# Two layers with causal attention on one core: row sums and values in one product, and the maxima on ScalarE's queue

## The chip, the core and the metric

The kernel runs on 1 core of one Trainium2 chip. The metric is device time in microseconds (us), the median over runs of the whole program.

## What is computed

Two layers, each an attention-like part and a feed-forward part. The change touches only the first of these parts, causal attention over 8 sequences of 512 tokens with 16 heads (32 of each head's query elements, 16 of them rotated):

```
q = concat(q_sem, rope(q_geo));  k likewise;  v = x @ Wv.T
scores = einsum('bhqd,bhkd->bhqk', q, k) * scale
scores = where(causal, scores, finfo.min)
attn   = softmax(scores, axis=-1)
out    = einsum('bhqk,bhkd->bhqd', attn, v)  ->  reshape(B, S, 256) @ Wo.T
```

## The kernel before

The program is a row of phases (layer norm, attention, layer norm, feed-forward, gates, state space and so on), each with a block per engine and a barrier at its end. The phase of the change is `causal_attention`. Its work is cut into 16 **halves** (batch b, f = 0 or 1: 8 heads each), and a half into 4 steps t, one **pair** of heads per step. All engines run the same `step(b, f, t, n)` in the same order. The order is written by hand: the calls inside `step` are each engine's queue, and each engine works through it in order.

For one pair, the work runs as follows.

- **Scores and maxima**, two steps ahead. PE's `scores` (L374, L377) makes scores with the query on the partitions, in three fills j = 0, 1, 2 of `p_s`. DVE's `maximum` (L573) takes the negated row maxima. POOL splits them in two (L347, L349). One step ahead, DVE's `turn_maxima` (L587) transposes them, and SP's `maxima_out` (L267) writes them to DRAM; `maxima_in` (L277, four transfers) reads them back as extra rows of the query tile `qs`.
- **Scores again, turned**, in the pair's own step. PE's `turned_scores` (L384) has the key on the partitions, and the extra rows subtract the maximum. It also comes in three fills of one buffer `p_st`: turned fill j, then DVE's `keep_past` (L580, the causal edge), then ACT's `exponential` (L522) into `pt_a`, `pt_b` or `pt_c`, and only then turned fill j + 1. Fill 0 of the next pair waits for the third exponential and for the maxima.
- **Values**. For a quad (4 heads, two pairs) PE's `weigh` (L414) multiplies the exponentials by `v_pad` into `p_o`, and by `ones` into `p_sum`: 16 products each per quad, each into 32 of the 128 partitions. `v_pad` has a head's 16 values in 16 columns and zeros in the other 16; both quads of a half add into the same `p_o` and `p_sum`. Fill 0 comes at t = 1 (quad 0) and t = 3 (quad 1), fills 1 and 2 at t = 2 and at t = 0 of the next half.
- **Normalisation**. At t = 0 of the next half DVE takes two reciprocals of `p_sum` (L625, L633) and multiplies into `ot` (L636).
- **Output**. For a finished batch PE's `project_out` (L422) runs at t = 3 and t = 2 of the next batch's first half, and DVE adds the residual (L600).

Beside this PE projects q, k and v of later halves (L48 to L50), DVE and POOL rotate them (L594, L325, L329), ACT copies them (L527, L552, L543), and SP writes them to DRAM (`spread_rows`, L255) and reads them back stacked by head (`stack`, L262: two transfers of 384 KB for q at t = 0, two for k at t = 1).

## Time and profile before

| | us |
|---|---|
| median of 3 runs (6273.44 to 6284.51) | 6275.0 |
| the profiled execution, its own time | 6271.5 |
| its span in the trace | 6269.7 |
| attention: first to last product with `ot` | 162.1 to 795.5 |
| PE busy, whole span | 5619.0 (90%) |
| DVE busy | 4504.9 (72%) |
| ACT busy | 3469.1 (55%) |
| POOL busy | 3610.0 (58%) |

The shares are means over phases with different limits. The phase of the change is a tenth of the span, so it is read by its own stretch, from about 62 us to 804 us. In the trace a matmul of fp32 counts as two records, so 4 products stand as "x8".

### The profile page before, as it was taken

Reading aid. Unit: us, or ns where it says so; the run is one execution under the profiler, and the core shown is the slowest. Engines: PE = TensorE matmul, PEld = TensorE weight load, DVE = VectorE, ACT = ScalarE, POOL = GpSimd, SP = SyncE. Lnnn points to the kernel's source line nnn. Section 1 sums busy time; section 2 is a strip of 40 time slices with the busy share of each in tenths; the row PEclk is TensorE's granted clock in tenths of the full one; section 3 lists DMA queues with packets and bytes.
Section 4 is the critical chain, followed back from the end, with each engine's and each line's share of the span. In section 5 each row is a group of like instructions: output and inputs, shape, how many; then the busy total and the mean of one; then the engine's idle time right before and its main releaser. Section 6 shows DMA issues by size and latency. Waiting matters only on the chain. (4 is left out here: it accounts for less than half of the span.)

```text
span 6269.7 us, 129594 instructions
## 1 busy us (share of the span) xinstructions
PE 5619.0 (90%) x41820; PEld 4006.3 (64%) x41820; DVE 4504.9 (72%) x6855; ACT 3469.1 (55%) x4692; POOL 3610.0 (58%) x4085
## 2 busy tenths in 40 slices
PE   5888858747999999999999999999999999985599
PEld 3444447535777777777777777777777777763487
DVE  4666555545888888888888888888888888844444
ACT  2233222134777777777777777777777777731122
POOL 2111100005888888888888888888888888830000
PEclk8899779868999999999999999999999999987799
DMA  3333210122111111111111111111111111122100
GB/s 91 91 93 84 68 61 24 47 71 66 31 28 33 29 30 28 32 29 30 29 30 32 28 31 28 32 29 30 28 33 29 30 28 31 29 77 74 42 24 20
DMA packets 428605, 263.10 MB, mean 42 GB/s; under 512 B 264740, under 2 KB 359524, under 8 KB 427652
## 3 DMA queue, kind: packets, MB, share of 16 engines
q1 hardware_dynamic: 420100, 253.98, 15.7%
q10 hardware_dynamic: 8448, 8.39, 0.4%
...
## 5 line engine op out<-in xcount | busy, mean ns | idle before, releaser
L1537 ACT ACTIVATE ss_r<-ss_pssum,ss_eps 128x512 f32<-128x512 f32 x512 | 352.8, 689 | 900.5 <-PE ss_pssum L1468 900.5
L1597 DVE SCALAR_TENSOR_TENSOR ss_psb<-ss_psb,ss_norm,ss_r 128x512 f32<-128x512 f32 x512 | 362.8, 754 | 446.2 <-ACT ss_r L1539 446.2
L1468 PE MATMUL ss_pssum<-ss_sq,ss_pairssum 128*128 128x512 f32 x1024 | 570.9, 639 | 57.1 <-DVE ss_fr L1585 57.0
L1349 POOL TENSOR_TENSOR ss_sq<-ss_sq 128x512 f32<-128x512 f32 x256 | 329.7, 1288 | 452.5 <-ACT ss_sq L1546 452.5
L48 PE MATMUL ss_psb<-x_hi,ss_whi 128*128 x1024 | 529.5, 517 | 4.4 <-DVE ss_fr L1585 4.4
L1449 PE MATMUL ss_psse<-ss_rot 64*128 64x128 f32 x8224 | 529.4, 279 | 1.2 <-POOL ss_rot L1331 1.2
L1379 POOL TENSOR_TENSOR ss_own<-ident,ss_tk 128x512 f32<-128x512 f32 x512 | 524.8, 1047 | 0.0
L1449 PEld LDWEIGHTS ss_psse<-ss_rot 64*128 64x128 f32 x8224 | 480.1, 188 | 44.4 <-issue 42.9
L48 PE MATMUL ss_psc<-x_hi,ss_whi 128*128 x1024 | 504.9, 493 | 0.0
L50 PE MATMUL ss_psb<-x_hi,ss_wlo 128*128 x1024 | 404.1, 395 | 0.0
L49 PE MATMUL ss_psc<-x_lo,ss_whi 128*128 x1024 | 403.6, 394 | 0.0
L1339 POOL TENSOR_TENSOR ss_sq<-ss_sq 128x512 f32<-128x512 f32 x256 | 325.1, 1270 | 135.0 <-ACT ss_sq L1553 135.0
L50 PE MATMUL ss_psc<-x_hi,ss_wlo 128*128 x1024 | 402.2, 393 | 0.0
L49 PE MATMUL ss_psb<-x_lo,ss_whi 128*128 x1024 | 402.0, 393 | 0.0
L1304 POOL MEMSET ss_rot<- 128x4096 f32 x1 | 3.5, 3512 | 669.5 <-POOLq L2018 669.5
L1458 PE MATMUL ss_psm<-ss_xe,ss_bt 128*128 128x16 f32 x3084 | 388.9, 264 | 0.0
L1458 PEld LDWEIGHTS ss_psm<-ss_xe,ss_bt 128*128 128x128 f32 x3084 | 363.9, 191 | 31.2 <-issue 0.2
L1597 DVE SCALAR_TENSOR_TENSOR ss_psc<-ss_psc,ss_norm,ss_r 128x512 f32<-128x512 f32 x512 | 361.5, 752 | 0.0
L1619 DVE TENSOR_TENSOR ss_gm<-ss_psse,ss_dec 128x1024 f32<-128x1024 f32 x257 | 314.7, 1224 | 41.7 <-POOL ss_dec L1340 41.7
L1539 ACT ACTIVATE ss_r<-ss_r 128x512 f32<-128x512 f32 x512 | 324.1, 633 | 16.3
L1373 POOL TENSOR_TENSOR ss_rot<-ss_rot,ss_tmp 128x512 f32<-128x512 f32 x256 | 333.0, 1301 | 0.0
L1519 ACT ACT_TABLE_LOAD x257 | 329.7, 1283 | 4.5
...
## 6 DMA issues: line engine op xcount, KB each, us to landing
...
a_qs<-head_rows SPq DMA_DIRECT2D x32, 384.0 KB, 5.7
a_ks<-head_rows SPq DMA_DIRECT2D x32, 384.0 KB, 5.6
...
```

The costliest lines, as they stand in the source:

```text
L48: nc.tensor.matmul(out, w_hi, x_hi, start=first, stop=False)
L49: nc.tensor.matmul(out, w_hi, x_lo, start=False, stop=False)
L50: return nc.tensor.matmul(out, w_lo, x_hi, start=False, stop=last)
L1349: G.tensor_tensor(sq[:, 0, 0], sq[:, 0, 0], sq[:, 0, 1], ALU.add).then_inc(ss_b, 1)
L1373: G.tensor_tensor(rot[:, j, 0], rot[:, j, 0], tmp[:, 0, 0], ALU.add)
L1379: last = G.tensor_tensor(own[:, h * TPB:(h + 1) * TPB], g.ident[:].rearrange("p (o t) -> p o t", o=1).broadcast_to([P, TPB, P]), at_diagon ...
L1449: last = M(p_se[:, h * TPB + c, :], rot[at, 1 - j, e, cols], rot[at, 1 - j, 2 + e, cols], start=e == 0, stop=e == 1)
L1458: last = M(p_m[:, (c * 2 + e) * PW:(c * 2 + e + 1) * PW], bt[:, 2 if e else j, c, :], xe[:, 1 - j, c, :], start=True, stop=True)
L1468: M(p_sum[:], pairs_sum[:], sq[:, q, 0], start=True, stop=True).then_inc((sum_b, sum_c)[q], 1)
L1519: A(trig[:, j, 0], fr[:], ACT.Sin, scale=UNDER_TURN)
L1537: A(r[:, q], p_sum[:], ACT.Ln, scale=1.0 / N1, bias=eps[:, 0:1]).then_inc(ln, 1)
L1597: link.mark(S(bank[:, e, :], bank[:, e, :], norm[:, 2 * q + e:2 * q + e + 1], r[:, q], ALU.mult, ALU.mult))
```

## The change

- `v_pad` is filled with ones where it was filled with zeros. One product then gives a head's values in 16 of its 32 partitions and its row sums in the other 16. The `ones` products and `p_sum` are gone, and each quad has its own `p_o` buffer.
- ACT's new `take` copies a quad's `p_o` twice to SBUF: plain (`o_sb`), and scaled by a column `own` of ones and zeros that keeps only the value rows (`o_own`). It comes at t = 3 for quad 0 and at t = 0 of the next half for quad 1.
- SP's new `gather_sums` moves the sum rows of `o_sb` by four transfers of 32 KB to the partitions that hold the values (`sums`).
- POOL adds the two `o_own` at t = 1 into `o_all`. DVE takes the first reciprocal at the end of t = 1, the second in t = 2 ahead of `keep_past` 2, and multiplies into `ot` at the end of t = 2.
- `maxima_out` and `maxima_in` move from SP's queue to ACT's, between exponentials 0 and 1. The four transfers in become two, of two rows each. DVE turns the maxima before `maximum` 0 and not after it.
- `stack` and `spread_rows` no longer stand behind the maxima on SP's queue.
- `project_out` moves from t = 3 and t = 2 of half f = 0 to t = 3 of f = 0 and t = 0 of f = 1. ACT's two copies into `v_pad` come before exponential 0.

```diff
         vt, v_pad = sb("vt", [P, SEQ]), sb("vpad", [P, TPB, 2, 2, 4, 2 * DH])
-        ones, nil = sb("ones", [P, 2, 2 * DH]), sb("nil", [P, 2, TPB])
+        nil = sb("nil", [P, 2, TPB])
+        o_sb, sums = sb("osb", [P, 2, SEQ]), sb("sums", [P, SEQ])
+        o_own, o_all = sb("oown", [P, 2, SEQ]), sb("oall", [P, SEQ])
+        strips, own = sb("strips", [P, 2, 4]), sb("own", [P, 2])
...
-        p_o, p_sum = ps("o", [P, SEQ]), ps("sum", [P, SEQ])
+        p_o = [ps(f"o{q}", [P, SEQ]) for q in range(2)]
...
             for t in range(4):
                 step(BATCH, 0, t, BATCH)
+            step(BATCH, 1, 0, BATCH)
...
-            def maxima_out(b, g_next):
-                p = g_next % 2
-                sp.wait_ge(turned_done, b * 8 + g_next + 1)
-                sp.dma_start(max_dram[p], trn[:, p, :]).then_inc(max_out[p], 16)
-
-            def maxima_in(b, g_next):
-                p = g_next % 2
-                f, u = g_next // 4 % 2, g_next % 4
-                sp.wait_ge(max_out[p], (b * 4 + g_next // 2 + 1) * 16)
-                columns = max_dram[p].rearrange("(a c) r -> c a r", a=TPB)
-                for e in range(2):
-                    for s in range(2):
-                        at = 64 * e + KS + s
-                        sp.dma_start(qs[at:at + 1, f, u, :].bitcast(FP32).rearrange("o (i a r) -> o i a r", i=TPB, a=TPB),
-                                     columns[8 * e + 4 * s:8 * e + 4 * s + 4].unsqueeze(0)).then_inc(max_in[p], 16)
+            def gather_sums(half, quad):
+                sp.wait_ge(o_copied, half * 2 + quad + 1)
+                for c in range(4):
+                    to, at = 32 * c + DH * quad, 32 * c + DH * (1 - quad)
+                    sp.dma_start(sums[to:to + DH, :], o_sb[at:at + DH, quad, :]).then_inc(sums_in, 16)
 
             def step(b, f, t, n):
...
                 half = 2 * n + f
                 after = (b, 1) if f == 0 else (b + 1, 0)
-                if is_pair(4 * half + t + 1):
-                    maxima_out(b, 4 * f + t + 1)
-                if t < 2 and is_half(half + 1):
-                    stack(*after, t)
-                if is_pair(4 * half + t + 1):
-                    maxima_in(b, 4 * f + t + 1)
                 if t == 0 and is_half(half + 1):
+                    stack(*after, 0)
                     spread_rows(*after, 1)
+                if t == 1 and is_half(half + 1):
+                    stack(*after, 1)
                 if t == 2 and is_half(half + 2):
                     spread_rows(b + 1, f, 0)
-                if f == 1 and t == 0 and 1 <= n < BATCH:
+                if t == 3 and is_half(half):
+                    gather_sums(b * 2 + f, 0)
+                if t == 0 and is_half(half - 1):
+                    gather_sums(b * 2 + f - 1, 1)
+                if f == 1 and t == 1 and 1 <= n < BATCH:
                     before = b - 1
...
-            G.memset(v_pad[:], 0.0).then_inc(cleared, 1)
+            G.memset(v_pad[:], 1.0).then_inc(cleared, 1)
...
+                if t == 1 and is_half(half - 1):
+                    pool.wait_ge(o_masked, (b * 2 + f) * 2)
+                    at_least(pool, ot_done, b * 2 + f - 1)
+                    G.tensor_tensor(o_all[:], o_own[:, 0], o_own[:, 1], ALU.add).then_inc(merged, 1)
...
-                    for psum, left in ((p_o, lambda c: v_pad[:, kt, f, quad, c, :]), (p_sum, lambda c: ones[:, quad, :])):
-                        for c in range(4):
-                            last = M(psum[32 * c:32 * c + 32, kt * P:SEQ], left(c), pt[:, c // 2, c % 2, at:at + width],
-                                     start=quad == 0 and j == 0, stop=quad == 1 and j == 2, skip_group_check=True)
+                    for c in range(4):
+                        last = M(p_o[quad][32 * c:32 * c + 32, kt * P:SEQ], v_pad[:, kt, f, quad, c, :], pt[:, c // 2, c % 2, at:at + width],
+                                 start=j == 0, stop=j == 2, skip_group_check=True)
...
-                outs = f == 0 and 1 <= n <= BATCH
+                outs = 1 <= n <= BATCH
...
-                if t == 3 and outs:
+                if f == 0 and t == 3 and outs:
                     if is_half(half + 1):
                         pe.wait_ge(vpad_done, b * 2 + f + 2)
                     pe.wait_ge(ot_done, b * 2)
-                    project_out(b, 1, c)
+                    project_out(b, 0, c)
                 if t == 3 and is_half(half + 2):
-                    if outs:
-                        pe.wait_ge(res_done, b * 2 - 1)
...
                 if earlier:
                     pe.wait_ge(exp_done, pairs_done * FILLS)
                     weigh(ef, eq, 2)
+                if f == 1 and t == 0 and outs:
+                    if is_half(half + 1):
+                        pe.wait_ge(rope_read, counts(1) + 4)
+                    pe.wait_ge(res_done, b * 2 - 1)
+                    project_out(b, 1, c)
                 if t == 1 and is_half(half + 2):
                     at_least(pe, rope_read, counts(1) + 4)
+                    if f == 1 and outs:
+                        pe.wait_ge(res_done, b * 2)
                     project(b + 1, f * HALF + P, c).then_inc(proj_done, 1)
-                if t == 2 and outs:
-                    if is_half(half + 2):
-                        pe.wait_ge(rope_read, counts(2) + 1)
-                    if is_half(half + 1):
-                        pe.wait_ge(vt_ready, b * 2 + f + 2)
-                    at_least(pe, res_done, b * 2 - 2)
-                    pe.wait_ge(ot_done, b * 2)
-                    project_out(b, 0, a)
                 if t == 3 and is_half(half + 2):
-                    if outs:
-                        pe.wait_ge(res_done, b * 2)
+                    if f == 0 and outs:
+                        pe.wait_ge(res_done, b * 2 - 1)
...
                     pe.wait_ge(exp_done, pairs_done * FILLS + 1)
                     if t == 1:
                         pe.wait_ge(vpad_done, b * 2 + f + 1)
-                        at_least(pe, ot_done, b * 2 + f)
+                    at_least(pe, o_masked, b * 4 + f * 2 - 1 + t // 2)
                     weigh(f, t // 2, 0)
...
+            def take(half, quad):
+                act.wait_ge(pv_done, (half * 2 + quad + 1) * FILLS)
+                at_least(act, rec_done, half)
+                at_least(act, merged, half)
+                A(o_sb[:, quad], p_o[quad][:], ACT.Copy).then_inc(o_copied, 1)
+                A(o_own[:, quad], p_o[quad][:], ACT.Copy, scale=own[:, quad:quad + 1]).then_inc(o_masked, 1)
+
+            def maxima_out(b, g_next):
+                p = g_next % 2
+                act.wait_ge(turned_done, b * 8 + g_next + 1)
+                act.dma_start(max_dram[p], trn[:, p, :]).then_inc(max_out[p], 16)
+
+            def maxima_in(b, g_next):
+                p = g_next % 2
+                f, u = g_next // 4 % 2, g_next % 4
+                act.wait_ge(max_out[p], (b * 4 + g_next // 2 + 1) * 16)
+                columns = max_dram[p].rearrange("(a c) r -> c a r", a=TPB)
+                for e in range(2):
+                    at = 64 * e + KS
+                    act.dma_start(qs[at:at + 2, f, u, :].bitcast(FP32).rearrange("s (i a r) -> s i a r", i=TPB, a=TPB),
+                                 columns[8 * e:8 * e + 8].rearrange("(s i) a r -> s i a r", s=2)).then_inc(max_in[p], 16)
...
-                if here:
-                    exponential(b, f, t, 0)
-                if t == 0 and is_half(half + 1):
-                    high(*after, 1)
-                if t == 2 and is_half(half + 2):
-                    high(b + 1, f, 0)
...
                 if t == 3 and is_half(half + 1):
                     act.wait_ge(vt_done, b * 2 + f + 2)
...
                 if here:
+                    exponential(b, f, t, 0)
+                if is_pair(4 * half + t + 1):
+                    maxima_out(b, 4 * f + t + 1)
+                if t == 0 and is_half(half + 1):
+                    high(*after, 1)
+                if t == 2 and is_half(half + 2):
+                    high(b + 1, f, 0)
+                if is_pair(4 * half + t + 1):
+                    maxima_in(b, 4 * f + t + 1)
+                if here:
                     exponential(b, f, t, 1)
                     exponential(b, f, t, 2)
+                if t == 3 and here:
+                    take(b * 2 + f, 0)
+                if t == 0 and is_half(half - 1):
+                    take(b * 2 + f - 1, 1)
...
-                V.tensor_tensor(rows, p_ab[part][:].rearrange("p (n d) -> p n d", n=2), rows, ALU.add).then_inc(res_done, 1)
+                V.tensor_tensor(rows, p_ab[1][:].rearrange("p (n d) -> p n d", n=2), rows, ALU.add).then_inc(res_done, 1)
...
-                outs = f == 0 and 1 <= n <= BATCH
+                outs = 1 <= n <= BATCH
                 here = is_half(half)
                 if here:
                     keep_past(b, f, t, 0)
+                if is_pair(4 * half + t + 1):
+                    turn_maxima(b, 4 * f + t + 1)
                 if ahead:
                     maximum(b, f, t, 0)
-                if is_pair(4 * half + t + 1):
-                    turn_maxima(b, 4 * f + t + 1)
-                if t == 3 and outs:
-                    add_residual(b, 1)
+                if f == 0 and t == 3 and outs:
+                    add_residual(b, 0)
                 if here:
                     keep_past(b, f, t, 1)
                 if t % 2 and is_half(half + 2):
...
                     maximum(b, f, t, 1)
                 if t % 2 and is_half(half + 2):
                     turn(b + 1, f, t // 2, 1)
-                if t == 0 and is_half(half - 1):
-                    dve.wait_ge(pv_done, (b * 2 + f) * 2 * FILLS)
-                    V.reciprocal(rec[:, 0:SEQ // 2], p_sum[:, 0:SEQ // 2])
+                if f == 1 and t == 0 and outs:
+                    add_residual(b, 1)
+                if t == 2 and is_half(half - 1):
+                    V.reciprocal(rec[:, SEQ // 2:SEQ], sums[:, SEQ // 2:SEQ]).then_inc(rec_done, 1)
                 if here:
                     keep_past(b, f, t, 2)
-                if t == 2 and outs:
-                    add_residual(b, 0)
                 if ahead:
                     maximum(b, f, t, 2)
-                if t == 0 and is_half(half - 1):
-                    V.reciprocal(rec[:, SEQ // 2:SEQ], p_sum[:, SEQ // 2:SEQ]).then_inc(rec_done, 1)
+                if t == 1 and is_half(half - 1):
+                    dve.wait_ge(sums_in, (b * 2 + f) * 128)
+                    at_least(dve, ot_done, b * 2 + f - 1)
+                    V.reciprocal(rec[:, 0:SEQ // 2], sums[:, 0:SEQ // 2])
+                if t == 2 and is_half(half - 1):
                     at_least(dve, wo_done, b * 2 if f else b * 2 - 2)
+                    dve.wait_ge(merged, b * 2 + f)
                     dve.wait_ge(rec_done, b * 2 + f)
-                    V.tensor_tensor(ot[:, 1 - f, :], p_o[:], rec[:], ALU.mult).then_inc(ot_done, 1)
+                    V.tensor_tensor(ot[:, 1 - f, :], o_all[:], rec[:], ALU.mult).then_inc(ot_done, 1)
 
             batches(dve, step)
```

Two places show how the queues move. First ACT, in the loop's second half (f = 1) at t = 0, from exponential 0 on (after, as far as the copies of `p_o`); `a_pta`, `a_ptb` and `a_ptc` are the outputs of exponentials 0, 1 and 2. Before:

```order
L522 ACTIVATE a_pta<-a_psst 128x1024 [waits a0_pv]
L525 REGISTER_ALU
L527 ACTIVATE a_yhi<-a_y 128x512 [waits a0_kspread,ln0_loaded6]
L518 REGISTER_ALU
L218 REGISTER_ALU [waits a0_keep]
L522 ACTIVATE a_ptb<-a_psst 128x1024 [waits a0_pv]
...
L522 ACTIVATE a_ptc<-a_psst 128x512 [waits a0_pv]
L550 REGISTER_ALU
L552 ACTIVATE a_vt<-a_psa 128x512 [waits ln0_normed,ln0_var]
```

After:

```order
L518 ACTIVATE a_pta<-a_psst 128x1024 [waits a0_pv]
L529 REGISTER_ALU
L530 DMA maxima<-a_trn 128x32 [waits a0_turned]
L543 REGISTER_ALU
L545 ACTIVATE a_yhi<-a_y 128x512 [waits a0_kspread,ln0_loaded6]
L539 DMA a_qs<-maxima 2x16x32 [waits a0_maxout1]
L539 DMA a_qs<-maxima 2x16x32
...
L518 ACTIVATE a_ptb<-a_psst 128x1024 [waits a0_pv]
...
L518 ACTIVATE a_ptc<-a_psst 128x512 [waits a0_pv]
L521 ISA
L524 ACTIVATE a_osb<-a_pso 128x512 [waits a0_merged,a0_rec,a0_pv]
L525 ACTIVATE a_oown<-a_pso,a_own 128x512
```

Exponential 1 now stands behind three DMA issues and a wait for the first of them to land, and two copies of `p_o` stand behind exponential 2.

Second SP, in the same half at t = 0. Before:

```order
L267 DMA maxima<-a_trn 128x32 [waits a0_turned]
L259 ISA
L262 DMA a_qs<-head_rows 48x4x512 [waits a0_qspread]
L262 DMA a_qs<-head_rows 48x4x512
L277 DMA a_qs<-maxima 1x16x32 [waits a0_maxout1]
L277 DMA a_qs<-maxima 1x16x32 x3
```

After, from `gather_sums` of the step before:

```order
L272 DMA a_sums<-a_osb 16x512 [waits a0_ocopied]
L272 DMA a_sums<-a_osb 16x512 x3
L263 ISA
L266 DMA a_qs<-head_rows 48x4x512 [waits a0_qspread]
L266 DMA a_qs<-head_rows 48x4x512
```

The maxima no longer follow the two stacked transfers on one queue.

## Rows read from the trace of the kernel before

**Rows 1.** The tile `a_ot`: the multiplication that ends each of the 16 halves

```profile
L636 DVE TENSOR_TENSOR a_ot<-a_pso,a_rec x16: 691/692/693, 162.1 to 795.5; 128x512 f32<-128x512 f32 x16
```

**Rows 2.** Stages: length, busy time (instructions) of PE, PEld, DVE, ACT, POOL; clock, DMA

```profile
162.00:795.50 633.50, 547.79 (x3862) 284.43 (x3862) 373.19 (x635) 184.42 (x244) 88.61 (x166) 0.87 0.34 81
```

**Rows 3.** Waits from 157 to 700 us: total, times, longest

```profile
PE a_psst L384 <- DMA a_qs<-maxima: 50.8, 26, 3.4
```

**Rows 4.** Timeline of PE, a step t = 0: start, length, instruction, idle before it

```profile
363.19 1.04 PE L414 MATMUL a_pssum<-a_pta,a_ones 128*32 128x512 f32 x8
...
364.17 0.50 PE L384 MATMUL a_psst<-a_qs,a_ks 50*128 50x512 f32 x2
...
366.34 0.83 PE L414 MATMUL a_pssum<-a_ptb,a_ones 128*32 128x384 f32 x8
366.98 0.40 PE L414 MATMUL a_pso<-a_ptb,a_vpad 128*32 128x128 f32 x8
367.20 0.40 PE L414 MATMUL a_pssum<-a_ptb,a_ones 128*32 128x128 f32 x8
367.53 0.50 PE L384 MATMUL a_psst<-a_qs,a_ks 50*128 50x384 f32 x4
...
369.06 0.61 PE L414 MATMUL a_pssum<-a_ptc,a_ones 128*32 128x256 f32 x8
370.03 0.39 PE L384 MATMUL a_psst<-a_qs,a_ks 50*128 50x256 f32 x2 [0.35 <-ACT a_ptb L522]
...
375.74 0.72 PE L384 MATMUL a_psst<-a_qs,a_ks 50*128 50x512 f32 x2 [3.20 <-DMA a_qs<-maxima]
```

**Rows 5.** Timeline of ACT, the same step

```profile
365.28 1.03 ACT L522 ACTIVATE a_pta<-a_psst 128x1024 f32<-128x1024 f32 x1 [1.98 <-DVE a_psst L580]
368.95 1.02 ACT L522 ACTIVATE a_ptb<-a_psst 128x1024 f32<-128x1024 f32 x1 [2.13 <-DVE a_psst L580]
372.07 0.60 ACT L522 ACTIVATE a_ptc<-a_psst 128x512 f32<-128x512 f32 x1 [2.09 <-DVE a_psst L580]
372.65 0.60 ACT L552 ACTIVATE a_vt<-a_psa 128x512 f32<-128x512 f32 x1
```

**Rows 6.** Timeline of DVE, the same step, and POOL's operation of the added one's size

```profile
366.90 1.28 POOL L329 TENSOR_TENSOR a_ylo<-a_y,a_yhi 128x512 fp32r<-128x512 f32 x1 [2.78 <-ACT a_yhi L527]
...
369.88 1.75 DVE L625 RECIPROCAL a_rec<-a_pssum 128x256 f32<-128x256 f32 x1
...
371.55 0.41 DVE L580 TENSOR_TENSOR a_psst<-a_psst,a_limit 128x256 f32<-128x256 f32 x1
```

**Rows 7.** Timeline of SP's queue, the same step (DMA issues)

```profile
367.30 0.32 SPq L267 DMA_DIRECT2D maxima<-a_trn  x1
367.75 0.83 SPq L262 DMA_DIRECT2D a_qs<-head_rows  x2
368.72 2.58 SPq L277 DMA_DIRECT2D a_qs<-maxima  x4
```

**Rows 8.** Timeline near the phase's end, with no stacked transfer in flight

```profile
775.19 0.32 SPq L267 DMA_DIRECT2D maxima<-a_trn  x1
776.62 2.55 SPq L277 DMA_DIRECT2D a_qs<-maxima  x4
...
780.71 0.21 PEld L384 LDWEIGHTS a_psst<-a_qs,a_ks 50*128 50x128 f32 x2 [1.42 <-DMA a_qs<-maxima]
```

**Rows 9.** Stages of 3 us around that step, columns as in rows 2

```profile
374.00:377.00 3.00, 1.26 (x6) 0.64 (x6) 1.33 (x3) 0.04 (x1) 0.00 (x0) 0.81 0.66 236
377.00:380.00 3.00, 3.00 (x11) 1.97 (x11) 1.41 (x3) 0.99 (x1) 0.00 (x0) 0.50 0.00 0
398.00:401.00 3.00, 1.93 (x11) 1.30 (x11) 1.84 (x4) 1.58 (x3) 0.35 (x2) 0.79 0.19 71
```

**Rows 10.** DMA issues: size and time from issue to landing

```profile
a_qs<-head_rows SPq DMA_DIRECT2D x32, 384.0 KB, 5.7
```

**Rows 11.** Timeline of PE, an output projection at full clock

```profile
393.89 1.99 PE L422 MATMUL a_psa<-a_wo,a_ot 128*128 128x256 f32 x8
```

19 lines of the change are left out of this document (11 added, 8 removed).

## The prediction

> **What bounds the kernel now.** I read the tile `a_ot` first, for the period. Its multiplication ends a half, and 16 of them lie between 162.1 and 795.5 us [rows 1]: 633.4 us for 15 periods, 42.2 us for a half of four steps. The stage's busy times come next [rows 2]: PE 547.8 of 633.5 us, DVE 373, ACT 184, POOL 89. Per half PE is busy for 547.8/15 = 36.5 us and idle for 5.7, at a mean granted clock of 0.87, between its levels 1.2 and 2.4 GHz. PE is the engine that the others wait for, and its idle time says what it waits for itself. The longest of it ends with a maxima transfer: 50.8 us in 26 waits from 157 to 700 us [rows 3], which is 26 waits in some 13 halves, two per half and 3.9 us.
>
> The timelines of one step t = 0 show why. I count from its start T = 364.17 [rows 4]. Turned fill 0 runs at T, exponential 0 ends at T + 2.14 [rows 5], turned fill 1 starts at T + 3.36, exponential 1 ends at T + 5.80, turned fill 2 starts at T + 5.86. The next step starts at T + 11.57, after 3.20 us of waiting for the maxima [rows 4]. On SP's queue [rows 7] the write of the maxima is issued at 367.30, two stacked transfers at 367.75, and the four transfers in from 368.72 to 371.30. They reach PE 4.44 us later (375.74). Near the phase's end nothing stacked is in flight, and the same transfers, issued until 779.17, release PE at 780.71 [rows 8]: 1.54 us. So the stacked transfers, 5.7 us to land [rows 10], hold up the small ones behind them by 2.9 us. After such a wait the clock falls: 0.81, then 0.50 in the next stretches [rows 9]. A busy share of only 1.93 in 3 us already goes with 0.79 [rows 9].
>
> **The sums leave PE.** Per quad they are four groups of products. By start to next start they take 0.98 (363.19 to 364.17), 0.64 (366.34 to 366.98) and 0.33 us (367.20 to 367.53), and the last at most 0.61 [rows 4]: 2.56 in all. A tenth or so of each group is its drain, which the values' products then show instead, so I take 2.3 per quad, 4.6 per half at full clock. Divided by the clock of 0.87 it would be 5.3. I take 4.8. PE busy per half: 36.5 − 4.8 = 31.7 us.
>
> **The maxima on ACT's queue.** ACT now stands still from exponential 0 to exponential 1. From the write's issue to the first issue in it was 1.42 us (367.30 to 368.72) and 1.43 [rows 7, 8]. An issue in takes 2.58/4 = 0.64 [rows 7], so two take 1.29. The block is B = 2.71 us. The trace shows no two-row issue; a stacked one takes 0.42 [rows 7], so the pair lies between 0.83 and, if the price goes by rows, 2.58: B between 2.25 and 4.0. I take 2.71, since the form is nearest to the old one. The turning comes before `maximum` 0 now, so the write needn't wait for it. ACT's copy `y_hi` lies inside the wait.
>
> In the step above exponential 1 can start at T + 2.14 + 2.71 = T + 4.85, against T + 4.78 before, and turned fill 2 at T + 5.93. PE reaches that point at 5.51 without its wait of 0.35, less the sums of 0.97 and 0.5: T + 4.04. So **1.9 us of the freed PE time turns into a wait for ACT**. What follows: keep 0.41 and exponential 0.60 end by T + 7.5, where they ended at 8.50 behind the reciprocal of 1.75 [rows 5, 6]. PE's rest of the step is 2.5 us, so it ends at T + 8.45. The maxima are issued by T + 4.85 and land 1.54 later if nothing holds them up: the wait of 3.2 is gone.
>
> Step t = 2 has the same chain and the same idle of 1.9. The first reciprocal, at the end of t = 1, delays its `keep_past` 0 by about 1.1 (1.75 against a gap of some 0.65); the second fits into DVE's slack. At t = 1 and t = 3 projections keep PE busy until turned fill 2, and the later exponential costs some 0.15 each. One of two output projections, 1.93 us [rows 11], moves into the idle time of t = 0 in every second half: −0.95 per half. PE idle per half: 1.9 + 1.9 + 1.1 + 0.3 − 0.95 = 4.25.
>
> **What else is added.** Four copies of `p_o` per half, 0.60 each [rows 5], stand behind exponential 2 at t = 0 and t = 3 (1.2 us, at t = 0 with `a_vt` 1.8). The next exponential 0 is needed 1.1 us after the next T, which lies about 1 us after exponential 2: it is hidden, and costs up to 0.8 per step if steps get as short as 7.5. POOL's addition, 1.28 us [rows 6] on an engine that is busy for 89 us of 633, is hidden before `total`. If it weren't, the rotation of q would be late, not the chain. The gathers are 4 issues (1.7 us) and a landing on SP, and are waited for at the end of t = 1, some 4 us later; if late, all of DVE stands behind that wait. The moved stacked transfer of k waits for the gather at the end of t = 0 and is issued at about 1.4 us into t = 1, where it was 3.4 before, and needed only at t = 2.
>
> **The sum.** Period: 31.7 + 4.25 = 35.95 us, 6.25 less. Over 15 periods that is −94. Half 0 ahead of them gives −6. The tail gets longer: copy 0.6, issues 1.7, landing 1.5, less the last sums: +3. In all −97, from 6271.5 (the profiled execution) to 6174.5. The median of the runs is 3.5 above that execution, so **6178 us**. Changes within 0.2% (12.5 us) can't be told from none.
>
> **Rivals.**
>
> *The clock comes back too.* At full clock in all of the stage, 36.5 us of busy time is about 0.87 × 36.5 = 31.8, less 4.6 = 27.2, plus 4.25 = 31.4: −160. Halfway there is 6145. For: the waits of 3.2 go. Against: idle shares of 4.25 in 36 are hardly below 5.7 in 42, and rows 9 show a fall after less. Chance 0.14.
>
> *The maxima stay late on their new queue.* If the landing of 4.44 us stays wherever a stacked transfer is in flight (t = 0 and t = 1), the maxima are there at T + 9.3, 0.8 after the end of t = 0 and 1.5 after that of t = 1 (about 7.75 long). That is 2.3 per half, +35: 6213. For: ACT's queue has no engines of its own in any row, and stacks go out before the maxima now. Against: the landing of 1.54 is that of transfers with an empty queue before them. The Trainium skill (DMA: Bandwidth & Descriptors, Issuing engines are not separate DMA queues) says that DMAs of all queues run on the same 16 engines and interleave, and that another queue only saves issue time. By that rule the time would be this rival's; the trace of before has these transfers on one queue only and can't tell. The same page (Why a DMA increments its semaphore by 16 and not by 1) says that a transfer spreads over as many engines as divide its slowest dimension. That would be 2 for the two-row form, and points the same way; no run here shows it yet. Chance 0.12.
>
> *ACT is blocked for longer.* A step of the bare chain takes 2.14 + B + 1.08 + 1.6 = 4.84 + B. With B = 4.3 the steps are 10.0 (with the projection of v), 9.15, 10.25 and 9.15, with 0.3 for the outputs: 38.9 per half, −50, so 6222. Chance 0.09.
>
> *The change is slower, by the same place.* The chain rules all steps then: a half is 21.7 + 4B us, which is 42.2 from B = 5.1 on. With B = 6, when the write of the maxima lands behind the stacked transfers as these land themselves (5.7 us less what has passed), 45.7 per half give +54: 6330. For: the stacked transfers are now issued just ahead of that write. Against: at 2 of 4 steps nothing is in flight, and B of 1.42 + issues was the same in both places of [rows 7, 8]. Chance 0.07.
>
> *The removed products buy nothing* (PE only waits longer) and the gain is the maxima's 3.9 us alone: 6275 − 58 = 6217. Against: PE has no wait at t = 1 and t = 3 before turned fill 2. Chance 0.04.
>
> **How the numbers follow.** The forecast, 6150 to 6205, has 0.54. The range of 6120 to 6232 takes in most of the faster clock and the three weaker gains. Faster by over 0.2%: 0.54 + 0.14 + 0.12 + 0.09 + 0.04 = 0.93, less 0.01 for a weak case that ends near no change. Slower has 0.06 of the 0.07, same 0.02.
>
> **What would show it.** Right: no `a_pssum` rows; 36 us between `a_ot` rows; maxima waits on PE far below 50.8 us; PE waiting for `a_ptb` at t = 0 and t = 2 for about 1.9 us each; exponential 1 about 2.7 us after the end of exponential 0. Wrong: an issue of the two-row transfer above 1 us, 1.42 grown to over 2, maxima waits at t = 0 and t = 1, or DVE waiting for `a_sums`. The forecast falls if B is over 3.5 us or the granted clock leaves 0.87 by more than 0.05.

## The result, and the profile after

| | median us | lowest to highest | runs |
|---|---|---|---|
| before | 6276.06 | 6273.44 to 6284.51 | 4 |
| after | 6235.38 | 6233.29 to 6247.79 | 4 |

The ratio is 0.9936, 95% interval 0.9924 to 0.9949: 40.7 us faster, where 97 were forecast. The time lies above the range of 6120 to 6232. The profiled execution of after is the slowest of its four runs: its own time is 6247.8 us, its span 6245.8. Against the profiled execution of before (6271.5) that is only 23.7 us less, so the readings below explain 23.7 us and not 40.7.

The tile `a_ot` of after and the stage between its first and last multiplication (length, then busy time and instructions of PE, PEld, DVE, ACT, POOL; clock, DMA share, GB/s):

```profile
L667 DVE TENSOR_TENSOR a_ot<-a_oall,a_rec x16: 679/681/693, 175.2 to 768.0; 128x512 f32<-128x512 f32 x16
```

```profile
175.20:768.00 592.80, 515.00 (x2806) 270.62 (x2806) 362.73 (x614) 211.12 (x298) 109.84 (x177) 0.76 0.38 89
```

That is 592.8/15 = 39.5 us, against 42.2 [rows 1], at a clock of 0.76 in place of 0.87. But the two stages don't hold the same work. `a_ot` is now made two steps later in the half: its first multiplication comes 13.1 us later and its last 27.5 us earlier, so the stage of after leaves out two full steps at its start and takes in two nearly empty ones at its end. The stage from the first exponential 0 to the last, 63 steps or 15.75 halves, is the same stretch of the work in both, but for the products taken out. Before, then after:

```profile
112.48:781.75 669.27, 581.43 (x4074) 303.14 (x4074) 397.51 (x678) 198.22 (x264) 97.46 (x184) 0.88 0.35 84
112.94:752.07 639.13, 563.77 (x3084) 296.48 (x3084) 398.00 (x678) 230.80 (x324) 121.83 (x199) 0.77 0.39 93
```

| per half, us | before | after |
|---|---|---|
| length | 42.5 | 40.6 |
| PE busy | 36.9 | 35.8 |
| PE idle | 5.6 | 4.8 |
| clock of the stage | 0.88 | 0.77 |
| busy time times clock | 32.5 | 27.6 |

So a thousand TensorE instructions fewer are only 1.1 us per half less busy time. Busy time times clock fell by 4.9: the work did leave, and most of what it freed came back as slower products.

What PE waited for in after, 157 to 700 us (total, times, longest), the row of [rows 3] and its neighbours:

```profile
PE a_psst L383 <- DMA a_qs<-maxima: 26.2, 17, 2.8
PE a_psst L383 <- ACT a_ptb L518: 24.3, 21, 3.7
PE a_psst L383 <- ACT a_ptc L518: 7.1, 10, 0.8
```

The waits for maxima halved (50.8 in 26 before). In their place stand waits for exponential 1. A step t = 0 of after on PE, where [rows 4] were read before (start, length, instruction, idle before it):

```profile
357.38 0.50 PE L383 MATMUL a_psst<-a_qs,a_ks 50*128 50x512 f32 x2
...
359.88 0.50 PE L383 MATMUL a_psst<-a_qs,a_ks 50*128 50x384 f32 x4
...
361.07 0.64 PE L412 MATMUL a_pso<-a_ptc,a_vpad 128*32 128x256 f32 x8
362.68 0.39 PE L383 MATMUL a_psst<-a_qs,a_ks 50*128 50x256 f32 x2 [0.97 <-ACT a_ptb L518]
...
364.81 0.63 PE L50 MATMUL a_psa<-x_hi,a_wlo 128*128 x1
...
367.57 0.50 PE L383 MATMUL a_psst<-a_qs,a_ks 50*128 50x512 f32 x2 [0.90 <-DMA a_qs<-maxima]
```

The same step on ACT and, below, on SP's queue (issues have a q):

```profile
358.51 1.02 ACT L518 ACTIVATE a_pta<-a_psst 128x1024 f32<-128x1024 f32 x1 [0.58 <-DVE a_psst L608]
358.59 0.36 ACTq L530 DMA_DIRECT2D maxima<-a_trn  x1
...
360.13 1.28 ACTq L539 DMA_DIRECT2D a_qs<-maxima  x2
361.60 1.02 ACT L518 ACTIVATE a_ptb<-a_psst 128x1024 f32<-128x1024 f32 x1 [1.55 <-DVE a_psst L608]
```

```profile
357.37 2.43 SPq L272 DMA_DIRECT2D a_sums<-a_osb  x4
360.28 0.82 SPq L266 DMA_DIRECT2D a_qs<-head_rows  x2
```

The step is 367.57 − 357.38 = 10.2 us long, 11.57 before. Turned fill 2 waits 0.97 us for exponential 1. The write of the maxima is issued 0.08 us after exponential 0 starts, not at its end, so exponential 1 starts 2.07 us after that end (359.53). The two reads of the maxima are issued in 1.28 us, until 361.41, and reach PE at 367.57, which is 6.16 us later. SP was held by the gathers, so the stacked q goes out at 360.28, into the same time.

The clock after such short waits is the main reading. The stretches around one step, columns as in rows 2, and the waits there:

```profile
336.00:339.00 3.00, 3.00 (x26) 1.08 (x23) 3.00 (x6) 0.53 (x2) 1.07 (x3) 1.00 0.00 0
340.00:342.80 2.80, 1.55 (x16) 0.58 (x17) 2.42 (x4) 1.32 (x2) 1.28 (x1) 0.96 0.12 41
342.80:346.00 3.20, 3.20 (x13) 1.79 (x14) 2.74 (x4) 1.21 (x3) 0.78 (x2) 0.50 1.00 324
346.00:350.00 4.00, 4.00 (x14) 2.58 (x14) 1.83 (x4) 1.07 (x2) 0.00 (x0) 0.50 0.15 47
350.00:354.00 4.00, 4.00 (x14) 2.40 (x13) 2.49 (x4) 1.02 (x1) 0.00 (x0) 0.50 0.01 1
```

```profile
339.83 0.51 PE L383 MATMUL a_psst<-a_qs,a_ks 50*128 50x384 f32 x4 [0.41 <-ACT a_pta L518]
...
342.80 0.58 PE L383 MATMUL a_psst<-a_qs,a_ks 50*128 50x256 f32 x2 [1.25 <-ACT a_ptb L518]
...
348.19 0.63 PE L49 MATMUL a_psa<-x_lo,a_whi 128*128 x1
348.62 0.63 PE L50 MATMUL a_psa<-x_hi,a_wlo 128*128 x1
...
369.40 0.40 PE L49 MATMUL a_psa<-x_lo,a_whi 128*128 x1
369.64 0.39 PE L50 MATMUL a_psa<-x_hi,a_wlo 128*128 x1
```

The clock is full from 336 us on. Two waits of 0.41 and 1.25 us come, with work between them, and then at least 11 us at 0.50 in which PE never stops. The projections of the step run in them: a projection product takes 0.63 us and the next starts after 0.43, where it is 0.40 and 0.24 at full clock (369.40). By that ratio the 11.2 us (342.80 to 354.00) would be 6.3 at full clock, so I estimate that some 5 us go for 1.7 us of waiting, if nothing else would have held the step up. Not each wait does this: after the one of 0.41 the clock stayed at 0.96 up to the next wait. The Trainium skill (TensorE: Matmul & The Clock Gate, A second HAM failure mode: psum-queue depth-cycling) tells of a kernel whose clock oscillates since PE is idle for short times between its groups of matmuls, often enough. This trace agrees, with 1.00, 0.96 and 0.50 in the stretches above.

### The profile page after: what moved, and what is told of

Same layout as the page of the kernel before. It is cut to its first block and busy times, and to the rows that moved or that the text cites. A ratio compares the mean times of both kernels' runs of the same rounds, so it can differ in the third digit from the quotient of the medians.

```text
span 6245.8 us, 127791 instructions
## 1 busy us (share of the span) xinstructions
PE 5602.4 (90%) x40796; PEld 4001.3 (64%) x40796; DVE 4506.1 (72%) x6856; ACT 3504.9 (56%) x4756; POOL 3632.0 (58%) x4101
## 5 line engine op out<-in xcount | busy, mean ns | idle before, releaser
L1404 POOL TENSOR_TENSOR ss_rot<-ss_rot,ss_tmp 128x512 f32<-128x512 f32 x256 | 332.7, 1300 | 0.0
L1405 POOL TENSOR_TENSOR ss_rot<-ss_rot,ss_tmp 128x512 f32<-128x512 f32 x256 | 332.5, 1299 | 0.0
```

Source lines behind the costliest of these rows:

```text
L1404: G.tensor_tensor(rot[:, j, 0], rot[:, j, 0], tmp[:, 0, 0], ALU.add)
L1405: G.tensor_tensor(rot[:, j, 1], rot[:, j, 1], tmp[:, 0, 1], ALU.add).then_inc(rot_b, 1)
```

## The experiments

Eighteen kernels ran, 0.2% (12.5 us) again being what can be told. "before" was run beside each (its medians lie between 6274.9 and 6277.8). PE's waits, busy times and clocks below are of the stretch from 162 to 700 us where nothing else is said; for after that is 478.16 us busy at 0.78, for before 474.05 at 0.89.

One correction holds for several expectations. The phase has 16 halves (the 16 multiplications of `a_ot`), and the expectations of e9 and e12 count 28 to 32. The sums' products are 4.6 x 16 = 74 us of PE work, e12 and e13 leave out 60% of that, 44 us, and the time at which "work off is time off" would put e12 is 6230. The sixteen zero-weight products per place are 1.93 us long there at full clock, 62 us in all over 32 places (e16's row below), and not 1.03 each time as e16's expectation says.

**e1_zeros_back.** PE's work as before, in the new order.

```diff
-                    for c in range(4):
-                        last = M(p_o[quad][32 * c:32 * c + 32, kt * P:SEQ], v_pad[:, kt, f, quad, c, :], pt[:, c // 2, c % 2, at:at + width],
-                                 start=j == 0, stop=j == 2, skip_group_check=True)
+                    for left in (lambda c: v_pad[:, kt, f, quad, c, :], lambda c: zero[:]):
+                        for c in range(4):
+                            last = M(p_o[quad][32 * c:32 * c + 32, kt * P:SEQ], left(c), pt[:, c // 2, c % 2, at:at + width],
+                                     start=j == 0 and first, stop=j == 2, skip_group_check=True)
+                        first = False
```

> The changed kernel, and behind each group of value products the same number of products with weights of zero into the same place: PE does as much work as before the change, the result stays. Theory (the clock): removing the sums' products left PE too idle in places and the clock fell from 0.87 to 0.78 in this phase, which ate the saving. Then the granted clock of the phase returns to 0.85 or more and the time stays within 15 us of the changed kernel's 6235, or falls. Rival (PE's work counts and the clock falls for another reason, such as ACT's block): the clock stays near 0.78 and the time rises by the products' 4.6 us per half or more, 75 us, to 6310.

Measured: 6247.3 us (6242.9 to 6251.5), ratio 0.9952, interval 0.9939 to 0.9966. The clock is 0.91, PE's busy time 479.4 us. Putting back 74 us of PE work costs 12 us against after, which is within what can't be told from nothing, and brings the clock back from 0.78. This is the pair that puts back exactly what the change took.

**e2_fill_wait.** 16 zero-weight products of 256 columns ahead of fill 2 of the values, at t = 0 and t = 2, where PE waits next for exponential 1.

```diff
+            def fill_wait(quad):
+                for _ in range(4):
+                    for c in range(4):
+                        M(p_o[quad][32 * c:32 * c + 32, 2 * P:SEQ], zero[:], pt_c[:, c // 2, c % 2, :],
+                          start=False, stop=False, skip_group_check=True)
...
                     pe.wait_ge(exp_done, pairs_done * FILLS)
+                    fill_wait(eq)
                     weigh(ef, eq, 2)
```

> The changed kernel, and 16 products of 256 columns with weights of zero only at t = 0 and t = 2, before fill 2 of the values, where PE waits 1.25 us for exponential 1; some 1.8 us of PE at full clock. Theory (the clock falls in the stretches after that wait): the clock of the phase rises to 0.9, the slow stretches after t = 0 and t = 2 shrink, and the period goes from 39.5 to about 37 us: some 40 us less, 6195. Rival (ACT's block sets the period): the filler costs nothing and brings nothing, or costs up to 0.6 us twice per half: 6235 to 6255.

Measured: 6220.8 us (6218.6 to 6222.1), ratio 0.9909, interval 0.9894 to 0.9925. The clock is 0.88. More work on the busiest engine, and 14.6 us less than after; it lies between the two times that I had given.

**e3_max_sp.** The maxima back on SP, the write ahead of the stacked transfers and the read behind them as before, the rest as after.

```diff
-                act.dma_start(max_dram[p], trn[:, p, :]).then_inc(max_out[p], 16)
+                sp.dma_start(max_dram[p], trn[:, p, :]).then_inc(max_out[p], 16)
...
+                if is_pair(4 * half + t + 1):
+                    maxima_out(b, 4 * f + t + 1)
+                if t < 2 and is_half(half + 1):
+                    stack(*after, t)
+                if is_pair(4 * half + t + 1):
+                    maxima_in(b, 4 * f + t + 1)
```

> The changed kernel with the maxima back on SP's queue (write, stacked transfers, two two-row transfers in, as before); values and sums in one product and the spread normalisation stay. Theory of the maxima's queue: the waits for the maxima return to 3 to 4 us per half, ACT's block goes, PE idles more and the clock falls to 0.75 or less: 6255 to 6280, no better than before the change. Rival (the maxima on ACT cost more by the block than they gain): faster than 6235.

Measured: 6236.3 us (6226.9 to 6243.1), ratio 0.9932, interval 0.9919 to 0.9946: as after. My expectation missed. With the sums gone, taking the maxima back to SP, in the old order with the stacked transfers, makes no difference in sum. PE waits more for them (35.0 us from 162 to 740, after 26.2) and less for exponential 1 (17.7 against 25.6): what ACT's block costs is what SP's queue costs.

**e4_sibling.** Before, with the other half of the change: maxima on ACT and read by two transfers of two rows, turned ahead of `maximum` 0, stacks no longer behind them on SP, ACT's copies into `v_pad` ahead of exponential 0. Products with ones, the normalisation and the place of the output projections stay old. The main lines of the edit:

```diff
-                sp.dma_start(max_dram[p], trn[:, p, :]).then_inc(max_out[p], 16)
+                act.dma_start(max_dram[p], trn[:, p, :]).then_inc(max_out[p], 16)
...
-                    maximum(b, f, t, 0)
                     turn_maxima(b, 4 * f + t + 1)
+                    maximum(b, f, t, 0)
```

> The kernel before with the maxima on ACT's queue, the turning first and the stacked transfers free of them, but with the products by ones and the old normalisation. Theory (the clock): PE has its 4.6 us more per half, so its waits are short, the clock is above 0.87, and the time is 6230 to 6245, close to the changed kernel: the removed products gave next to nothing. Rival (the sums' removal is what gives the 41 us): 6265 or more.

Measured: 6218.6 us (6217.0 to 6231.1), ratio 0.9912, interval 0.9899 to 0.9926: 59 us off before (6277.8 in that comparison), and 17 us faster than the whole change. It is faster than I expected under either theory. So these edits alone bring more than the whole change, and the rest of it (the sums' part and the moved projections) costs time on top of them. In 162 to 740 us PE waits 0.3 us for maxima (before 55.4), 45.4 for exponential 1.

**e12_drop_sums.** Before, without the products with ones for key tiles 1 to 3. It is the forecast's first term by itself.

```diff
                     for psum, left in ((p_o, lambda c: v_pad[:, kt, f, quad, c, :]), (p_sum, lambda c: ones[:, quad, :])):
+                        if psum is p_sum and kt > 0:
+                            continue
```

> The kernel before with nothing changed but this: the products with ones are left out for key tiles 1 to 3 (768 of 1280 columns, so 60 percent of what the change takes off TensorE, 2.9 us of 4.8 per half); the sums then hold key tile 0 only. Order, waits, queues and normalisation stay. If work off TensorE comes off the period at an unchanged clock: 32 halves x 2.9, some 80 to 90 us less over 28 to 32 halves, 6190 to 6200. If the clock gives it back, as e1 and e2 suggest: 6255 to 6285, with a clock in 162 to 740 of 0.82 or less in place of 0.89.

Measured: 6295.1 us (6287.4 to 6295.9), ratio 1.0033, interval 1.0020 to 1.0046. 44 us of work are left out and the kernel is 20 us **slower**, more than even the clock theory gave it; its clock, 0.85, is above the 0.82 that I had named. PE waits and a stretch of e12 (waits of 157 to 700 us; PE's timeline; stages):

```profile
PE a_psst L384 <- DMA a_qs<-maxima: 68.6, 33, 4.6
PE a_psst L384 <- ACT a_ptb L524: 13.7, 19, 0.8
```

```profile
381.55 0.49 PE L384 MATMUL a_psst<-a_qs,a_ks 50*128 50x512 f32 x2 [3.90 <-DMA a_qs<-maxima]
...
384.67 0.63 PE L50 MATMUL a_psa<-x_hi,a_wlo 128*128 x1
```

```profile
377.00:381.50 4.50, 0.65 (x3) 0.19 (x1) 3.12 (x4) 1.09 (x2) 0.40 (x2) 1.00 1.01 251
381.50:385.00 3.50, 3.45 (x13) 2.19 (x14) 1.66 (x4) 1.02 (x1) 0.00 (x0) 0.56 0.02 9
385.00:389.00 4.00, 4.00 (x14) 2.20 (x14) 1.83 (x6) 0.85 (x1) 0.00 (x0) 0.50 0.59 105
389.00:392.00 3.00, 3.00 (x12) 1.64 (x10) 1.58 (x3) 0.17 (x1) 0.00 (x0) 0.50 0.86 130
```

The waits for maxima grew from 50.8 to 68.6 us, those for exponential 1 from 6.6 to 13.7: 25 us more of waiting in 13 of the 16 halves. The wait of 3.90 is followed by 10 us at half clock, and the clock of the stage fell from 0.89 to 0.85. The products with ones stood in the time in which the maxima are on their way.

**e5_stack_first and e6_stack_fill.** After, with the stacked transfers ahead of the gathers on SP (gathers at t = 0 and t = 1, and a wait for the last turned scores in place of the order that the gathers gave); e6 adds the products of e2.

```diff
                 if t == 0 and is_half(half + 1):
+                    at_least(sp, st_done, (b * 8 + 4 * f) * FILLS)
                     stack(*after, 0)
+                if t == 0 and is_half(half - 1):
+                    gather_sums(b * 2 + f - 1, 0)
...
+                if t == 1 and is_half(half - 1):
+                    gather_sums(b * 2 + f - 1, 1)
```

> The changed kernel with SP's issues of t=0 and t=1 in another order: the stacked transfers of q (384 KB) ahead of the gathers of sums, which move from t=3 and t=0 to t=0 and t=1. Theory A (part of what is missing is the collision of the late-issued stacked transfer with the maxima, because four gather issues of 0.61 us hold SP ahead of it): write to read-issue gaps on ScalarE's queue fall from up to 5.0 to about 1.5 us, TensorE's waits for maxima in 162 to 740 from 26 us to under 12 us, time 6215 to 6230. Theory B (only TensorE's clock decides; the waits for exponentials leave it at 0.76 to 0.78 whatever SP does): 6232 to 6240 and clock of 162 to 740 unchanged.

> The order of e5 together with the sixteen zero-weight products ahead of fill 2 of the values at t=0 and t=2 (e2, 6220.8 by itself). If transfers and clock are two separate losses, the gains add: about 15 us of the clock and what e5 brings, 6195 to 6215, with a clock of 0.88 or above in 162 to 740. If the two are the same loss (a wait that was filled cannot be shortened again): 6216 to 6224.

Measured: e5 6278.0 us (6269.3 to 6282.6), ratio 1.0002, interval 0.9993 to 1.0011; e6 6204.4 us (6200.6 to 6205.6), ratio 0.9886, interval 0.9871 to 0.9901. e5 is 43 us above after and neither theory had it; e6 lies in the 6195 to 6215 that I gave it, but not for the reason given, since e5 brings nothing that could be added. PE no longer waits for maxima at all from 162 to 740 us, and waits 63.6 us for exponential 1 (after 25.6). The same place of e5 on ACT, and on SP:

```profile
359.61 1.02 ACT L520 ACTIVATE a_pta<-a_psst 128x1024 f32<-128x1024 f32 x1
359.69 0.35 ACTq L532 DMA_DIRECT2D maxima<-a_trn  x1
...
364.73 1.28 ACTq L541 DMA_DIRECT2D a_qs<-maxima  x2
```

```profile
357.00 0.81 SPq L266 DMA_DIRECT2D a_qs<-head_rows  x2
```

From the write's end of issue to the read's issue pass 4.69 us, where it was 1.1: the write of 16 KB lands while the stacked 384 KB, issued 2.7 us ahead, are in flight, and ACT stands still until it has. In 13 of e5's 14 or so halves from 162 to 740 us there is one such gap of 4.3 to 4.95 us. In after there are three over 4 us in 57 steps (4.17 to 4.68), and each has a stacked k issued 0.01 to 0.16 us before the write; two more, of 3.36 and 3.48, have the four gathers just issued. Before the change no gap of 56 is over 1.23. One of after's three:

```profile
410.59 1.02 ACT L518 ACTIVATE a_pta<-a_psst 128x1024 f32<-128x1024 f32 x1 [1.84 <-DVE a_psst L608]
410.70 0.36 ACTq L530 DMA_DIRECT2D maxima<-a_trn  x1
415.23 1.26 ACTq L539 DMA_DIRECT2D a_qs<-maxima  x2
416.66 1.02 ACT L518 ACTIVATE a_ptb<-a_psst 128x1024 f32<-128x1024 f32 x1 [5.05 <-issue]
```

```profile
410.69 0.81 SPq L266 DMA_DIRECT2D a_ks<-head_rows  x2
```

The Trainium skill (DMA: Bandwidth & Descriptors, Issuing engines are not separate DMA queues) says that transfers of all issuing engines run on the same 16 engines and interleave. These rows agree: another engine's queue did not take the small transfer past the large one.

e6 shows the other half: the same order with 62 us of filler is 73.6 us faster than e5, at a clock of 0.93 against 0.76. It has as many gaps over 4 us as e5 (13), and e4 has twelve over 3 us, with a stacked transfer issued 3.5 to 5 us before, and both are faster than after. So a gap isn't dear by itself; it is dear where PE has little else to do.

**e7_zeros_stack.** e1 in the order of e5 (the edits of both, shown above).

> e1 (zero-weight products behind each group of values, TensorE's work as before, 6247.3) with the stacked transfers ahead of the gathers. e1 and the sibling form e4 (6218.6) have the same work on TensorE and differ by 29 us in how the normalisation is done and when. If the place of the gathers on SP explains that difference: 6215 to 6228. If it is the rest of the normalisation (ScalarE's copies of rows, the reciprocals and the earlier end of it): 6240 to 6250.

Measured: 6266.0 us (6254.7 to 6273.5), ratio 0.9983, interval 0.9973 to 0.9992: neither. Moving the gathers behind the stacks costs here too, 19 us over e1. So they are not cured by a new place. Set beside e6, it also shows that the place of PE work counts for more than its amount: both have the same order, e7 has 74 us of zero-weight products spread behind the groups of values, e6 has 62 us of them at the two waiting places, and e6 is 62 us faster.

**e9_sibling_late, e10_after_late, e11_zeros_late.** e4, after and e1 with the read of the maxima issued behind exponential 1. ACT then no longer waits for the write's landing between the exponentials.

```diff
-                    maxima_in(b, 4 * f + t + 1)
                     exponential(b, f, t, 1)
+                    maxima_in(b, 4 * f + t + 1)
                     exponential(b, f, t, 2)
```

> e4 (the kernel before with maxima on ScalarE's queue, turn first and stacked transfers freed, 6218.6) with the read of the maxima issued behind exponential 1 in place of ahead of it. It takes 1.3 us off the way to exponential 1, for which TensorE waits (45 us in 162 to 740 in e4). If exponential 1 is what binds there: 28 halves' shares of 15 to 30 us less, 6192 to 6208. Rival: the read lands 2.0 us later (one exponential) and TensorE waits for maxima again, 6215 to 6235.

> The changed kernel (6235.4) with only the read of the maxima moved behind exponential 1, so that nothing on ScalarE stands between exponential 0 and 1 but the short convert. This brought e4 22 us (6218.6 to 6196.1, e9). If ScalarE's hold costs the changed kernel as much, 6208 to 6222. If its loss is TensorE's clock alone, set by any short wait, 6228 to 6238, with a clock of 0.76 to 0.80 in 162 to 740.

> e10 with the zero-weight products behind each group of values (TensorE's work as before the change, 4.6 us per half more than e10). Against e9 (6196.1) it differs in the normalisation only: gathers, copies and reciprocals in two steps. If that part costs nothing once ScalarE is not held: 6193 to 6203, below e10. If it costs what e1 against e4 shows (29 us): 6220 to 6230. If work taken from TensorE is time taken from the kernel, it is 60 us above e10, near 6275.

Measured:

| | us | lowest to highest | ratio, 95% interval | PE's waits for maxima |
|---|---|---|---|---|
| e9 | 6196.1 | 6190.0 to 6205.6 | 0.9876, 0.9861 to 0.9891 | 23.1 in 13 |
| e10 | 6267.4 | 6254.1 to 6277.9 | 0.9986, 0.9978 to 0.9995 | 52.4 in 24 (162 to 740) |
| e11 | 6260.2 | 6253.1 to 6269.0 | 0.9975, 0.9965 to 0.9985 | 49.5 in 27 |

The later read brings e4 22 us, costs after 32 and e1 13. e9 lies in the range that I gave it, e10 and e11 lie outside all of theirs. Only the sibling form has slack in which the maxima may land later; in the changed form they were late already. e9 and e11 have the same work on PE and lie 64 us apart, and taking work off PE again bought nothing (e10 has 74 us less of it than e11 and is 7 us slower, which can't be told from nothing).

**e14_no_gather, e15_zeros_late_no_gather.** After and e11 without the transfers of the sums: the reciprocals read ones, so these kernels leave the softmax's division out. In place of the order that the gathers gave, SP waits for the last turned scores before it stacks q.

```diff
-                    gather_sums(b * 2 + f, 0)
...
-                    gather_sums(b * 2 + f - 1, 1)
...
-                    dve.wait_ge(sums_in, (b * 2 + f) * 128)
+                    dve.wait_ge(o_copied, (b * 2 + f) * 2)
```

> The changed kernel (6235.4) without the gathers: the 128 transfers of rows of sums are left out, the reciprocals read ones, so the normalisation is by 1; ScalarE's copies and everything else stay, and a wait keeps the stacked rows of q safe. If the gathers on SP (4 issues of 0.61 us each, ahead of the stacked transfers at t=0) are what makes the changed form 17 to 29 us slower than the sibling form: 6200 to 6215. If it is the thinner work on TensorE: 6230 to 6255, with a clock below 0.80 in 162 to 740.

> e11 (zero-weight products back, read of the maxima behind exponential 1; 6260.2) without the gathers. e9 has the same work on TensorE and takes 6196.1. If the gathers explain the 64 us: 6190 to 6210, and the write-to-read gaps over 5 us are gone. If ScalarE's copies and the merge on POOL carry them: 6240 to 6262.

Measured: e15 6211.4 us (6204.9 to 6214.7), ratio 0.9894, interval 0.9877 to 0.9911; e14 6250.2 us (6240.6 to 6255.2), ratio 0.9952, interval 0.9936 to 0.9967. The gathers are worth 49 of the 64 us between e11 and e9 (e15), and the waits for maxima fall from 49.5 in 27 to 15.3 in 15. What remains, 15 us, is the copies, the merge, the two steps and the moved projections, taken together. In the thin form of e14 it doesn't help: the stacked transfers leave at once, as in e5, exponential 1 is waited for 50.8 us, and the clock is 0.76. It is 15 us slower than after. My expectation on ACT's gaps was half right: the longest in e15 is 7.7 us, 7.9 in e11, with an exponential inside both.

**e13_late_drop, e16_sibling_late_fill.** Work taken from e9 (the edit of e12) and added to it (that of e2).

> e9 (sibling form, read of the maxima behind exponential 1; 6196.1) with the products with ones left out for key tiles 1 to 3, as in e12, sums of key tile 0 alone. The same question as e12 where the maxima are fresher: if TensorE's work there only covers the way of the maxima and keeps the clock, 6205 to 6235 and a clock under 0.88; if its removal pays once the maxima come in time, 6130 to 6160.

> e9 (6196.1) with the sixteen zero-weight products ahead of fill 2 of the values at t=0 and t=2 (1.03 us each time, 66 us in all), of which e2 made 14.6 us and e6 over e5 73 us. If e9 still loses time to waits that lead to half clock: 6175 to 6190. If its waits lie elsewhere (the maxima at t=1 and t=3) and the clock is high already at 0.93, the products add up to their own length: 6196 to 6240.

Measured: e13 6187.0 us (6177.1 to 6187.9), ratio 0.9849, interval 0.9834 to 0.9864; e16 6230.2 us (6224.8 to 6231.5), ratio 0.9920, interval 0.9906 to 0.9934. The added products of e16, one place:

```profile
367.80 1.93 PE L404 MATMUL a_pso<-a_ptc,a_zero 128*32 128x256 f32 x32
```

Where the maxima come sooner, PE work has a price with the right sign: 62 us more cost 34. That 44 us less bring 9 is too little to be told from nothing, and e13 lies between its two expectations. So less than its own length, still. In e13 the waits for exponential 1 are 19.6 us, in e9 10.2, and those for maxima 29.0 against 23.1.

**e8_in_late, e17_late_no_fill, e18_late_half_fill.** e6 with the later read (the edit of e9); the same without filler; the same with eight products per place:

```diff
             def fill_wait(quad):
-                for _ in range(4):
+                for _ in range(2):
```

> e6 (stacked transfers ahead of gathers, zero-weight products ahead of fill 2 of the values; 6204.4) with the read of the maxima issued behind exponential 1 in place of ahead of it. In e6 the time from the write's issue to the read's on ScalarE sums to 132 us over 57 steps (61.5 us over 56 before) and TensorE waits 40 us for exponential 1: ScalarE is held by the write's landing. If that hold binds: the waits for exponential 1 fall under 15 us and the time to 6180 to 6195. Rival: the later read gives it back as waits for maxima, 6198 to 6210.

> e8 (6191.2) without its zero-weight products, nothing else changed: stacked transfers ahead of the gathers, read of the maxima behind exponential 1. It is the cleanest pair for the question of TensorE's clock in the changed form: 66 us of TensorE work less. If work off TensorE is time off: 6125 to 6160. If the clock and the waits take it back as in e2 against the changed kernel, and e6 against e5: 6225 to 6275, clock of 162 to 700 under 0.82 (0.91 in e8).

> e8 with eight zero-weight products per place in place of sixteen (33 us in all in place of 66). If the filler's size must cover the waits at t=0 and t=2, half of it leaves some of them: between e17 and e8, 6200 to 6230. If half is enough to keep the clock, it is the best of this form: 6165 to 6188.

| | PE work added | us | lowest to highest | ratio, 95% interval | clock | waits for maxima |
|---|---|---|---|---|---|---|
| e17 | 0 | 6221.7 | 6213.7 to 6224.2 | 0.9913, 0.9899 to 0.9926 | 0.80 | 36.3 in 22 |
| e18 | 31 | 6193.2 | 6180.9 to 6204.0 | 0.9863, 0.9848 to 0.9878 | 0.86 | 34.8 in 25 |
| e8 | 62 | 6191.2 | 6185.0 to 6193.7 | 0.9864, 0.9850 to 0.9878 | 0.91 | 19.1 in 18 (157 to 700) |

e17 fell a little below what the clock theory expected (6225 to 6275) and far from 6125 to 6160. Half the filler brings 28.5 of the 30.5 us; its time lies between the two that I gave e18.

### Pairs that differ in PE's work alone

| from, to | work at full clock | time |
|---|---|---|
| before, e12 | −44 | +20.2 |
| e9, e13 | −44 | −9.1 |
| after, e1 | +74 | +11.9 |
| e10, e11 | +74 | −7.2 |
| after, e2 | +62 | −14.6 |
| e5, e6 | +62 | −73.6 |
| e5, e7 | +74 | −12.0 |
| e17, e18 | +31 | −28.5 |
| e17, e8 | +62 | −30.5 |
| e9, e16 | +62 | +34.1 |

Four of these ten changes in time are under 12.5 us and can't be told from none. Of the other six, one has the sign of the change in work (e9, e16), at about half its size, and five have the other sign.

## Why the prediction was wrong

**The step that failed** is the first term, "I take 4.8. PE busy per half: 36.5 − 4.8 = 31.7". It set the removed products at the clock of 0.87 and let the rest of the work keep that clock. Measured are 35.8 us at 0.77. The work was priced rightly: busy time times clock fell from 32.5 to 27.6, 4.9 for my 4.6. At the old clock of 0.88 the 27.6 would be 31.3 us of busy time, so 4.5 us per half went to the slower clock, 4.5 x 16 = 72 us. The profiled execution was forecast at 6174.5 and took 6247.8, 73 us more (by the medians the miss is 57). (A product's length doesn't scale with the clock alone, so this is an estimate, from the two stages of exponential 0.) The prediction had named this as its own condition, that it falls if the clock leaves 0.87 by more than 0.05, and gave no chance to a fall. That the clock falls with the thin work is shown by after and e1, where the taken work alone is put back: 0.78 to 0.91. What the fall costs is shown by e5 and e6, e17 and e8, after and e2: PE has more to do and the kernel is faster, the clock up by 0.10 to 0.17.

I had the rival with the other sign of this, the clock coming back as the long waits go. I read [rows 9] as "after a wait of 3.2 us the clock falls", and took fewer and shorter waits for a better clock. In after waits of 0.97 to 1.25 us are already followed by half clock. That 0.79 went with a busy share of 1.93 in 3 us stood in rows 9, and I used it only against that rival.

**Point by point.**

- *The maxima on ACT's queue, B = 2.71.* The length was right in the typical step: 358.59 to 361.41 is 2.82 us, the two-row issue costs 0.64. Its start wasn't: I let the block begin when exponential 0 ends, and the write is issued 0.08 us after exponential 0 starts. Not right in all of them: the gap of 1.42 between issues grew to 4.5 where a stacked transfer left at the same moment, three times over 4 us in after. My point for the slower rival, "when the write of the maxima lands behind the stacked transfers", exists, and e5 is a kernel in which it happens in nearly each half; it is 43 us slower than after (its gathers were moved too).
- *Turned fill 2 waits 1.9 us at t = 0 and t = 2.* It was 0.97 and 1.25 in the steps shown, 24.3 us in 21 waits: 1.16 each. In the step t = 0 shown, exponential 1 starts at T + 4.22 in place of T + 4.85, since the block begins earlier, and PE gets to its wait at T + 4.33 in place of T + 4.04.
- *Idle per half 4.25.* Measured 4.8. The waits for maxima are a good part of it: 26.2 us from 157 to 700, 2 per half, where I said the wait is gone.
- *They land 1.54 later if nothing holds them up.* Something does in the step shown: 6.16 us. This is the rival "the maxima stay late on their new queue" (6213), with a chance of 0.12. It was half true, as the waits halved. e3 puts it plainly: with the sums gone, the old queue and order are as good. It was not the reason for what the change gained either; e4 gets its 59 us from the maxima on ACT, the turn ahead of `maximum` 0 and the freed stacks together, which weren't told apart.
- *What else is added.* Copies, POOL's addition and the reciprocals I set at nothing, and the gathers at 1.7 us of issue and a landing that nobody waits for. The landing was right: DVE waits for `a_sums` once, 7.6 us (below). The issue wasn't: four take 2.43 us, and their cost isn't their landing but what stands behind them on SP. I wrote that the stacked k goes out earlier than before, and left the collision out of the sum; only two rivals had it. In e11 and e15 the gathers are worth 49 us. Copies and merge are at most 15.
- *The tail, +3.* From the last exponential 0 to the last `a_ot` it is 15.9 us, 13.7 before, so +2.2.
- *The removed products buy nothing* (6217, chance 0.04). Nearest to what happened in its mechanism, and still too good: e4 without their removal is at 6218.6, and with it the kernel is at 6235.4.
- *Slips that change nothing.* Rows 11 show 1.99 us for an output projection, not 1.93, and the terms of the bare chain add up to 4.82, not 4.84.

```profile
L662 DVE RECIPROCAL a_rec<-a_sums x16: 1741/1743/1754, 163.9 to 764.5; 128x256 f32<-128x256 f32 x16
```

```profile
DVE a_rec L662 <- DMA a_sums<-a_osb: 7.6, 1, 7.6
```

The first row counts and dates the reciprocal that stands behind the gathers in after; the second is DVE's only wait for them, near the phase's end.

**What stays open.** Why the clock was 0.76 and not, say, 0.82 can't be derived from these runs; they only order it with the filler. Which of the sibling's edits carries its 59 us wasn't tried one by one, and no run reads the maxima in the one-row form on ACT's queue, so whether the two-row form lands later is open. And of the 15 us between e15 and e9, copies, merge, timing and the moved projections weren't separated.

**Better than both.** e9 is before with the sibling's edits and the read behind exponential 1: 6196.1 us. e8 keeps the change, with stacks first, the read late and zero-weight products: 6191.2 us. Their intervals (0.9861 to 0.9891, 0.9850 to 0.9878) overlap, so the two aren't told apart. Both are some 40 us faster than the change. Neither leaves anything out. Since e9 gets there with the products with ones in place of products with zeros, they seem to do the same service, and the simpler form is e9.
